# A second order for the loads and for TensorE's work ahead of a recurrence: W2's A2 quarters first, x's first rows in four batches between them, biases behind the products of W1

## The chip, the cores and the metric

The kernel runs on one core of a Trainium2 chip. The metric is the device time of one execution in microseconds (us), the median of several runs.

## The reference

x is 4 x 512 x 256 (batch, time, width), cond is 4 x 256, all f32. Cut to what matters:

```python
# layer 0: factors of rank 8 drawn from cond, one set for each batch row
c = (cond - mean) / sqrt(var + 1e-5) * ln_gamma + ln_beta
h = gelu(c @ W1 + bias1)                       # W1 256 x 256
w = h @ W2 + bias2                             # W2 256 x 8192 (8 MB)
a1, b1, a2, b2 = [t.reshape(B, 256, 8) for t in split(w, 4)]
u   = einsum('btd,bdr->btr', x, a2)
mid = gelu(x @ base_down + einsum('btr,blr->btl', u, b2))
v   = einsum('blr,btl->btr', b1, mid)
x2  = 2 * x + mid @ base_up.T + einsum('bkr,btr->btk', a1, v)
# layer 1: a recurrence over 512 steps
h_t = tanh(x2_t @ Wx + b + h_(t-1) @ Wh)       # h_(-1) = cond
out = x2 + h
```

## The kernel before

Each engine runs a program written out by hand in one order, and the programs meet at semaphores. There are two phases. The prologue builds all that the first step of the recurrence needs: the factors a2, b2, b1, a1 and the first 64 rows of time (T0) of x for all four batch rows, carried as far as x2 for the first 16 (the first 32 soon behind). The recurrence then runs 512 steps, each some 20 small TensorE products of the state with Wh in three bf16 parts (`state_products`), two tanh on ScalarE (ACT) and four small subtractions on VectorE (DVE). Later rows of x and the later blocks of layer 0 are worked in between the steps.

In the prologue, DMA loads are issued by SyncE (SP) in the order of its program. W2 is loaded in 16 quarters of types of 512 KB: type j (A1, B1, A2, B2), half c, and k, the half of the contraction. `w_products(j, c)` multiplies one half of one type: four products of 32 columns for k = 0, four for k = 1, each k behind its load's semaphore. Ahead of it a `bias_product(j, c)` puts bias2 into the same PSUM bank. The right-hand side `gRep` is gelu(c @ W1 + bias1), repeated for the ranks: it comes from the transposes of `cn` (the normalised cond), the copy `cT`, the products with W1 into `hpre`, two gelu on ACT, and a copy on DVE.

Behind each half DVE runs `keep_rank` (`wmul`, then `fac`), and `spread` makes b2d and a1d of it; A2 and B1 are turned by TensorE (`turn_factor`) and copied out as a2T and b1T. x's first rows are transposed (`first_transposes`) and copied by ACT to xT, and multiplied with base_down (`base_down_product`); u, the b2 product (out of b2d), gelu to mid0, base_up (`base_up_product`), v (`v0_product`), the a1 product (`a1_first_product`) and `make_x2` follow. `first_input_product` multiplies the first tile of x2 with Wx, and the last of them release the first tanh.

`keep_busy(n)` issues n products with zeros into columns that nobody reads; they stand where TensorE would otherwise wait. GpSimd (POOL) splits b, Wh and Wx into bf16 parts in that order (`parts`), each behind its load.

Of the kernel before, what the change touches and what calls it, by code (L numbers as in the profile page):

```python
# [32 lines left out]
def adaptive_lowrank_then_recurrence(nc, x, cond, base_up, base_down, ln_gamma, ln_beta, W1, bias1, W2,  # L33
# [24 lines left out]
    with ExitStack() as ctx:  # L58
# [16 lines left out]
        x_sb = sb("x_sb", [P, B, NTT, D])  # L75
# [69 lines left out]
        ld_x = [sem(f"ld_x{n}") for n in range(NTT)]  # L145
        ld_x_more = sem("ld_x_more")
# [74 lines left out]
        PLACE = {A2: 0, B2: 2, B1: 0, A1: 2}  # L221

        def wbank(j, c):
            return bank[PLACE[j] + c][:, 0:HC]
# [6 lines left out]
        def hpre(m):  # L231
            return (bank[7], bank[3])[m][:, D + B * m:D + B * (m + 1)]
# [61 lines left out]
        @block.sync  # L294
        def _(sp):
            w2v = W2.rearrange("(k p) (j n) -> k p j n", p=P, j=NTYPE)

            def load_x(n):
                sp.dma_start(x_sb[:, :, n], x[:, P * n:P * (n + 1)].rearrange("b p d -> p b d")).then_inc(ld_x[n], 16)

            def load_w2(j):
                for c in range(2):
                    for k in range(K2):
                        sp.dma_start(w2_sb[:, k, j, 2 * CH * c:2 * CH * (c + 1)],
                                     w2v[k, :, j, 2 * CH * c:2 * CH * (c + 1)]).then_inc(ld_w2[j][c][k], 16)
# [11 lines left out]
            sp.dma_start(x_sb[T0:P, :, 0], x[:, T0:P].rearrange("b p d -> p b d")).then_inc(ld_x_more, 16)  # L317
# [74 lines left out]
        def _(act):  # L392
# [3 lines left out]
            act.dma_start(bias1_sb[:], bias1.rearrange("(o n) -> o n", o=1)).then_inc(ld_bias1, 16)  # L396
            act.dma_start(b_rows[:], b_rnn.partition_broadcast(NPART)).then_inc(ld_b, 16)
            act.dma_start(bias2_sb[:], bias2.rearrange("(j c e n) -> e j c n", j=NTYPE, c=2, n=HC)).then_inc(ld_bias2, 16)
# [9 lines left out]
            for k in range(K2):  # L408
                act.wait_ge(tr_ready, k + 1)
                nc.scalar.copy(xT[:, k, :, 0:T0], bank[6 - k][:, 0:B * T0].rearrange("p (b t) -> p b t", b=B)).then_inc(  # L410
                    tr_moved, 1)
            for m in range(K2):
                act.wait_ge(hpre_ready, m + 1)
                nc.scalar.activation(gT[:, m, :], hpre(m), ACT.Gelu).then_inc(g_ready, 1)
            act.wait_ge(a2T_psum, 1)
# [29 lines left out]
            def fill_more_rows(h):  # L445
                act.wait_ge(rows_psum, h + 1)
                nc.scalar.copy(xT[:, :, 2 * h:2 * h + 2, T0:P],
                               more_rows_out(h).rearrange("p (k b t) -> p k b t", k=K2, b=2)).then_inc(rows_moved, 1)
# [40 lines left out]
        def _(dve):  # L489
            steps = [0]  # L490

            def then_wait(ins):
# [23 lines left out]
                                  bank[2][:, 0:K2 * B]).then_inc(cT_ready, 1)  # L516
# [126 lines left out]
        def _(pe):  # L643
            zeros_h = zeros[:].bitcast(BF16)
            pe.wait_ge(pool_step, 1)
            def keep_busy(n, spare=0):
                for _ in range(n):
                    nc.tensor.matmul(bank[spare][:, D:2 * D], zeros_h[:, 0:P], zeros_h[:, 0:D], start=True, stop=True,  # L648
                                     skip_group_check=True)

            keep_busy(WARM)
# [6 lines left out]
            keep_busy(12)  # L658

            def bias_product(j, c):  # L660
                nc.tensor.matmul(wbank(j, c), quadrant[:].rearrange("e i q -> e (i q)"),  # L661
                                 bias2_sb[:, j, c], start=True, stop=False, skip_group_check=True)
# [14 lines left out]

            def w_products(j, c):
                for k in range(K2):
                    pe.wait_ge(ld_w2[j][c][k], 16)  # L680
                    for e in range(NCH):
                        last = nc.tensor.matmul(wbank(j, c)[Q * e:Q * (e + 1), :],  # L682
                                                gRep[:, k].rearrange("p b r -> p (b r)"),
                                                w2_sb[:, k, j, HC * (NCH * c + e):HC * (NCH * c + e + 1)], start=False,
                                                stop=(k == K2 - 1), skip_group_check=True)
                last.then_inc(w_ready[j], 1)
# [24 lines left out]
            pe.wait_ge(ld_x[0], 16)  # L711
            first_transposes(0)
            first_transposes(1)
            keep_busy(4)
            pe.wait_ge(ld_bias1, 16)
            pe.wait_ge(h_ready, 2)
            for m in range(K2):
                nc.tensor.matmul(hpre(m), bias1_sb[:, P * m:P * (m + 1)], ident[0:1, 0:1].broadcast_to([1, B]),
                                 start=True, stop=False, skip_group_check=True)
            pe.wait_ge(cn_ready, 1)  # L720
            for k in range(K2):
                last = nc.tensor.transpose(bank[2][:, B * k:B * (k + 1)], cn[:, P * k:P * (k + 1)],
                                           ident[0:B, 0:B])
            last.then_inc(cT_psum, 1)
            keep_busy(4)
            pe.wait_ge(ld_down, 16)
            base_down_product(0, 0)
            pe.wait_ge(ld_w1, 16)
            pe.wait_ge(cT_ready, 1)
            for m in range(K2):  # L730
                for k in range(K2):
                    last = nc.tensor.matmul(hpre(m), w1_sb[:, k, P * m:P * (m + 1)], cT[:, k, :], start=False,
                                            stop=(k == K2 - 1), skip_group_check=True)
                last.then_inc(hpre_ready, 1)
            base_down_product(0, 1)
            for k in range(K2):
                base_down_product(1, k)
# [6 lines left out]
            bias_product(B2, 0)  # L744
            w_products(A2, 1)
            bias_product(B2, 1)
            keep_busy(4, 7)
            w_products(B2, 0)
            pe.wait_ge(fac_ready[A2], 2)
            turn_factor(A2, a2T_psum)  # L750
            for c in range(2):
                bias_product(B1, c)
# [5 lines left out]
            w_products(B2, 1)  # L758
            pe.wait_ge(ld_up, 16)
# [10 lines left out]
            w_products(B1, 0)  # L770
            for c in range(2):
                bias_product(A1, c)
# [5 lines left out]
            w_products(B1, 1)  # L778
            keep_busy(7, 7)
# [73 lines left out]
            def turn_more_rows(h):  # L853
                if h == 0:
                    pe.wait_ge(ld_x_more, 16)
                    pe.wait_ge(x2_next, 2)
                for k in range(K2):
                    for b in range(2):
                        e = 2 * k + b
                        last = nc.tensor.transpose(more_rows_out(h)[:, T0 * e:T0 * (e + 1)],  # L860
                                                   x_sb[T0:P, 2 * h + b, 0, P * k:P * (k + 1)], ident[T0:P, T0:P])
                last.then_inc(rows_psum, 1)

            def turn_rows(tile):
                n, b = unit_of(tile)
                if b == 0:
                    pe.wait_ge(ld_x[n], 16)
                for k in range(K2):
                    last = nc.tensor.transpose(rows_out(tile)[:, P * k:P * (k + 1)], x_sb[:, b, n, P * k:P * (k + 1)],  # L869
# [39 lines left out]
            def recurrence(pair, first, last):  # L909
                for s in range(PAIR):  # L910
# [6 lines left out]
                    else:  # L917
                        for m in range(K2):
                            first_input_product(0, m, 1).then_inc(z_ready, 1)
                        first_input_product(1, 0, 1)  # L920
                        bias_start(0, 1, 1)
                        for k in range(K2):
                            first_input_product(1, 1, k)
# [23 lines left out]

            pe.wait_ge(fac_ready[B1], 2)
            turn_factor(B1, b1T_psum)
            pe.wait_ge(bp_ready, 1)  # L950
# [5 lines left out]
            pe.wait_ge(b1T_ready, 2)  # L956
            for k in range(K2):
                v0_product(k)
            w_products(A1, 0)
            keep_busy(6, 7)  # L960
# [3 lines left out]
            w_products(A1, 1)  # L964
# [4 lines left out]
            bias_start(0, 1, 0)  # L969
            first_input_product(1, 0, 0)  # L970
            keep_busy(8, 7)
            pe.wait_ge(a1d_ready, 2)
            a1_first_product(1)
            keep_busy(3, 7)
# [26 lines left out]
```

## Time and profile before

| | us |
|---|---|
| median of three runs (526.53, 528.21, 528.35) | 528.21 |
| the profiled execution's own time | 527.65 |
| its span, first to last instruction | 525.9 |
| the prologue in it: to the products that release the first tanh | 37.6 |
| TensorE busy, as the profile shows it | 505.6 (96%) |
| DVE busy | 291.8 (55%) |
| ACT busy | 175.2 (33%) |

The device time lies 1.75 us above the span. TensorE's matmuls overlap, so that its busy share says only that few gaps stand between starts. Nearly all of the span is the recurrence, whose code the change leaves as it is but for its first step and the two transposes of more rows of x.

### The profile page before, as it was taken

The page shows a single profiled execution, that of the slowest core. Times are in us where ns is not written, and L with a number is a line of the kernel's source. Part 1 is how long each engine was busy: PE and PEld are TensorE (multiplying, and loading weights), DVE is VectorE, ACT ScalarE, POOL GpSimd, SP SyncE. Part 2 cuts the span into 40 slices and gives each one's busy share as a digit, 9 for nine tenths or more (in the row PEclk, how much of TensorE's full clock was granted, in tenths as well). Part 3 has the DMA queues.
Part 4 walks back from the last instruction along what each step waited for, and adds up shares of the span by engine and source line. Part 5 has one row for each costly group of instructions (what it writes and reads, how often), then busy time and mean ns, then how long its engine had stood idle before and what let it go on. Part 6 is the DMA issues. An engine that isn't in the chain of part 4 may idle for free.

```text
span 525.9 us, 33134 instructions
## 1 busy us (share of the span) xinstructions
PE 505.6 (96%) x14756; PEld 471.9 (90%) x14756; DVE 291.8 (55%) x2272; ACT 175.2 (33%) x1158; POOL 22.2 (4%) x35
## 2 busy tenths in 40 slices
PE   9999999999999999999999999999999999998885
PEld 6569999999999999999999999999999999998884
DVE  2535565565556556555655555555655655565553
ACT  3103333333333333333333333333333333333322
POOL 7350000000000000000000000000000000000000
PEclk9999999999999999999999999999999999999999
DMA  8970000000000000000000000000000000000000
GB/s 292 401 213 4 4 14 4 4 14 4 14 5 14 6 7 11 4 14 4 15 4 14 4 6 14 4 14 4 14 4 5 14 4 15 4 14 3 14 6 11
DMA packets 8114, 16.05 MB, mean 31 GB/s; under 512 B 500, under 2 KB 5924, under 8 KB 7972
## 3 DMA queue, kind: packets, MB, share of 16 engines
q1 hardware_dynamic: 7904, 13.90, 7.8%
q8 instruction: 115, 1.88, 1.5%
q14 instruction: 27, 0.22, 0.1%
q10 hardware_dynamic: 68, 0.05, 0.0%
HBM read 11.85 MB, written 2.10 MB: 27 GB/s over the span
## 4 chain that ended last, share of the span: by engine, by line
PE 94%; ACT 3%; issue 1%; DVE 1%; DVEq 0%; POOL 0%; POOLq 0%
PE bank L881 64%; PE bank L801 7%; PE bank L845 4%; PE bank L826 3%; ACT h_ring L462 3%; PE bank L850 2%; PE bank L840 2%; PE bank L821 2%; PE bank L831 2%; PE bank L648 2%; PE bank L682 2%; PE bank L810 1%; PE bank L661 1%; PE bank L785 1%; PE bank L869 1%
## 5 line engine op out<-in xcount | busy, mean ns | idle before, releaser
L881 PE MATMUL bank<-h_ring,whp 128*128 128x52 bf16 x6132 | 243.3, 186 | 13.2 <-ACT h_ring L462 13.2
L544 DVE TENSOR_TENSOR r_ring<-h_ring 128x4 f32<-128x4 f32 x1022 | 136.6, 164 | 205.7 <-ACT h_ring L462 203.2
L462 ACT ACTIVATE h_ring<-bank 128x4 f32<-128x4 f32 x1024 | 142.1, 174 | 320.3 <-PE bank L881 312.5
L881 PE MATMUL bank<-r_ring,whp 128*128 128x52 bf16 x4096 | 220.5, 185 | 0.0
L881 PEld LDWEIGHTS bank<-h_ring,whp 128*128 128x128 bf16 x6132 | 187.9, 96 | 34.2 <-ACT h_ring L462 25.8
L881 PEld LDWEIGHTS bank<-r_ring,whp 128*128 128x128 bf16 x4096 | 174.6, 96 | 0.0
L881 PE MATMUL bank<-l_ring,whp 128*128 128x52 bf16 (+1 forms) x2048 | 157.4, 178 | 0.0
L548 DVE TENSOR_TENSOR l_ring<-r_ring 128x4 bf16<-128x4 f32 x1024 | 136.2, 162 | 0.0
L881 PEld LDWEIGHTS bank<-l_ring,whp 128*128 128x128 bf16 x2048 | 122.5, 96 | 0.0
L801 PE MATMUL bank<-xp,wxp 128*128 128x32 bf16 x1488 | 63.0, 176 | 0.0
L801 PEld LDWEIGHTS bank<-xp,wxp 128*128 128x128 bf16 x1488 | 50.5, 96 | 0.0
L845 PE MATMUL bank<-mid,upT 128*128 128x128 f32 x120 | 28.1, 316 | 0.0
L826 PE MATMUL bank<-xT,down_sb 128*128 128x128 f32 x112 | 26.2, 316 | 0.0
L785 PE MATMUL bank<-ones,b3h 128*128 128x32 bf16 x128 | 22.4, 176 | 0.0
L845 PEld LDWEIGHTS bank<-mid,upT 128*128 128x128 f32 x120 | 17.9, 188 | 0.0
L826 PEld LDWEIGHTS bank<-xT,down_sb 128*128 128x128 f32 x112 | 16.7, 188 | 0.0
L592 DVE TENSOR_TENSOR y_sb<-x2T,h_ring 128x64 f32<-128x64 f32 x64 | 15.4, 283 | 0.6 <-ACT h_ring L462 0.6
L840 PE MATMUL bank<-mid,b1T 128*128 128x128 f32 x60 | 14.0, 316 | 0.0
L850 PE MATMUL bank<-v_sb,a1d 128*128 128x128 f32 x60 | 14.0, 316 | 0.0
L821 PE MATMUL bank<-xT,a2T 128*128 128x128 f32 x56 | 13.1, 316 | 0.0
L831 PE MATMUL bank<-u_sb,b2d 128*128 128x128 f32 x56 | 13.1, 316 | 0.0
L648 PE MATMUL bank<-zeros 128*128 128x256 bf16 x72 | 12.0, 319 | 1.0 <-POOL zeros L338 1.0
(123 smaller groups left out, 240.4 us busy)
## 6 DMA issues: line engine op xcount, KB each, us to landing
w_sb<-in_L_cond_W SPq DMA_DIRECT2D x16, 512.0 KB, 11.5
out<-o_sb SPq DMA_DIRECT2D x16, 128.0 KB
x_sb<-in_x SPq DMA_DIRECT2D x3, 512.0 KB, 15.2
x_sb<-in_x SPq DMA_DIRECT2D x2, 256.0 KB, 9.6
w_sb<-in_L_cond_W SPq DMA_DIRECT2D x1, 256.0 KB, 3.6
down_sb<-in_L_cond_base_down SPq DMA_DIRECT2D x1, 256.0 KB, 5.0
wh_sb<-in_L_cond_Wh SPq DMA_DIRECT2D x1, 256.0 KB, 11.1
up_sb<-in_L_cond_base_up SPq DMA_DIRECT2D x1, 256.0 KB, 11.3
```

The costliest lines, as they stand in the source:

```text
L462: nc.scalar.activation(h_ring[:, m, slot(pair, s), 0:B], zt, ACT.Tanh).then_inc(h_ready, 1)
L544: nc.vector.tensor_tensor(r_ring[:, k, q, 0:B], state_before(pair, s, k)[:, 0:B], state_hi_before(pair, s, k)[:, 0:B], ALU.subtract).then_ ...
L548: nc.vector.tensor_tensor(l_ring[:, k, q, 0:B], r_ring[:, k, q, 0:B], r_hi[:, k, q, 0:B], ALU.subtract).then_inc(l_ready, 1)
L785: nc.tensor.matmul(zbank(p, q, m)[:, 0:TC // 2], b3h[:, P * m:P * (m + 1)], ones[:], start=True, stop=False, skip_group_check=True)
L801: nc.tensor.matmul(zb, wxp[w][:, k, P * m:P * (m + 1)], rhs, start=False, stop=False, skip_group_check=True)
L821: ins = nc.tensor.matmul(columns(fill_out(tile, 0)), a2T[:, k].rearrange("p e q -> p (e q)"), xT[:, k, :, t0:t0 + BL], start=(k == 0), sto ...
L826: nc.tensor.matmul(columns(fill_out(tile, 1 + c)), down_sb[:, k, P * c:P * (c + 1)], xT[:, k, :, t0:t0 + BL], start=(k == 0), stop=False)
L831: nc.tensor.matmul(columns(fill_out(tile, 1 + c)), b2d[:, P * c:P * (c + 1)], u_sb[:], start=False, stop=True).then_inc(fmid_psum, 1)
L840: ins = nc.tensor.matmul(columns(fill_out(tile, 0)), b1T[:, k].rearrange("p e q -> p (e q)"), rhs, start=(k == 0), stop=(k == K2 - 1))
L845: nc.tensor.matmul(columns(fill_out(tile, 1 + c)), upT[:, k, P * c:P * (c + 1)], rhs, start=(k == 0), stop=False)
L850: nc.tensor.matmul(columns(fill_out(tile, 1 + c)), a1d[:, P * c:P * (c + 1)], v_sb[:], start=False, stop=True).then_inc(fup_psum, 1)
L881: return nc.tensor.matmul(zbank(p, q, m)[:, col0:col0 + n], whp[part][:, k, P * m:P * (m + 1)], rhs[:, 0:n], start=False, stop=stop, skip_ ...
```

## The change

The loads: W1 is now first, and laid out so that a partition takes two rows of W1 that lie together (the transposes of cn take every second column to match). The four quarters of A2 follow, each with one 64 KB batch of x's first rows behind it (`xa_sb`, 32 partitions for a batch row, two rows of time in each). Then come down, Wh, B2, up, Wx, B1, A1, and x's rows 64 to 127 (`xb_sb`). Before, x's first rows came first, then W1, down, A2, B2, Wh, up, B1, Wx, A1. On ACT's queue bias2's load stands ahead of b's.

```diff
-            sp.dma_start(x_sb[0:T0, :, 0], x[:, 0:T0].rearrange("b p d -> p b d")).then_inc(ld_x[0], 16)
-            sp.dma_start(w1_sb[:], W1.rearrange("(k p) n -> p k n", p=P)).then_inc(ld_w1, 16)
+            sp.dma_start(w1_sb[:], W1.rearrange("(p k) n -> p k n", p=P)).then_inc(ld_w1, 16)
+            for b in range(B):
+                load_w2_half(A2, b // 2, b % 2)
+                sp.dma_start(xa_sb[T0 // 2 * b:T0 // 2 * (b + 1)], x[b, 0:T0].rearrange("(q r) d -> q r d", r=2)).then_inc(
+                    ld_xa, 16)
             sp.dma_start(down_sb[:], base_down.rearrange("(k p) n -> p k n", p=P)).then_inc(ld_down, 16)
-            load_w2(A2)
+            sp.dma_start(wh_sb[:], Wh.rearrange("(k p) n -> p k n", p=P)).then_inc(ld_wh, 16)
             load_w2(B2)
-            sp.dma_start(wh_sb[:], Wh.rearrange("(k p) n -> p k n", p=P)).then_inc(ld_wh, 16)
             sp.dma_start(up_sb[:], base_up.rearrange("(k p) n -> p k n", p=P)).then_inc(ld_up, 16)
+            sp.dma_start(wx_sb[:], Wx.rearrange("(k p) n -> p k n", p=P)).then_inc(ld_wx, 16)
             load_w2(B1)
-            sp.dma_start(wx_sb[:], Wx.rearrange("(k p) n -> p k n", p=P)).then_inc(ld_wx, 16)
             load_w2(A1)
...
             def first_transposes(k):
-                for b in range(B):
-                    last = nc.tensor.transpose(bank[6 - k][:, T0 * b:T0 * (b + 1)], x_sb[0:T0, b, 0, P * k:P * (k + 1)],
-                                               ident[0:T0, 0:T0])
+                for r in range(2):
+                    last = nc.tensor.transpose(bank[6 + k][:, P * r:P * (r + 1)], xa_sb[:, r, P * k:P * (k + 1)],
+                                               ident[:])
```

On TensorE x's transposes move from before the products of W1 to behind A2's second half, and the products with base_down behind them, on both sides of A2's turning. The products with bias1 stand behind W1's, B2's second bias stands ahead of A2's second half, and the biases of B1 and A1, which now have columns of their own in the banks of A2 and B2, go ahead of A2's turning (the last of them just behind it). base_up's products come straight behind the b2 products; B1's two halves follow them. `w_half_products` splits a half at k: fillers or other products stand between. The fillers change in number at most places. ACT does its two gelu ahead of x's two copies.

The first place is TensorE's program from the first fillers on. zeros marks fillers, ident,x_sb (after: ident,xa_sb) x's transposes, ident,bias_sb bias1, ident,cn the transposes of cn, cT,w_sb the products with W1, xT,down_sb those with base_down, bias_sb,quadrant bias2, and w_sb,gRep those with W2. Before:

```order
L648 MATMUL bank<-zeros 128x256 x12
L669 MATMUL bank<-ident,x_sb 128x64 x8
L648 MATMUL bank<-zeros 128x256 x4
L718 MATMUL bank<-ident,bias_sb 128x4 x2
L722 MATMUL bank<-ident,cn 128x4 x2
L648 MATMUL bank<-zeros 128x256 x4
L675 MATMUL bank<-xT,down_sb 128x256
L732 MATMUL bank<-cT,w_sb 128x4 x4
L675 MATMUL bank<-xT,down_sb 128x256 x3
L661 MATMUL bank<-bias_sb,quadrant 128x256 x2
L682 MATMUL bank<-w_sb,gRep 32x256 x8
```

And now:

```order
L662 MATMUL bank<-zeros 128x256 x11
L730 MATMUL bank<-ident,cn 128x4 x2
L662 MATMUL bank<-zeros 128x256 x3
L739 MATMUL bank<-cT,w_sb 128x4 x2
L743 MATMUL bank<-ident,bias_sb 128x4
L739 MATMUL bank<-cT,w_sb 128x4 x2
L743 MATMUL bank<-ident,bias_sb 128x4
L662 MATMUL bank<-zeros 128x256
L674 MATMUL bank<-bias_sb,quadrant 128x256 x2
L694 MATMUL bank<-w_sb,gRep 32x256 x8
```

Eight transposes and four products with base_down have left the stretch ahead of W2's first products.

The second place is TensorE's program from A2's second half to the u product (xT,a2T). ident,fac is the turning of A2. Before, between A2's two halves stands one bias product, and behind the second:

```order
L661 MATMUL bank<-bias_sb,quadrant 128x256
L648 MATMUL bank<-zeros 128x256 x4
L682 MATMUL bank<-w_sb,gRep 32x256 x8
L691 MATMUL bank<-ident,fac 32x128 x8
L661 MATMUL bank<-bias_sb,quadrant 128x256 x2
L755 MATMUL bank<-xT,a2T 128x256 x2
```

Now:

```order
L682 MATMUL bank<-ident,xa_sb 128x128 x4
L674 MATMUL bank<-bias_sb,quadrant 128x256 x3
L688 MATMUL bank<-xT,down_sb 128x256 x2
L707 MATMUL bank<-ident,fac 32x128 x8
L688 MATMUL bank<-xT,down_sb 128x256 x2
L674 MATMUL bank<-bias_sb,quadrant 128x256
L694 MATMUL bank<-w_sb,gRep 32x256 x8
L774 MATMUL bank<-xT,a2T 128x256 x2
```

x's work and two more bias products have come in here.

The third place is from the turning of B1 (ident,fac) to the first a1 product (v_sb,a1d). mid,b1T is the v product; b3h, h_start, r_ring and l_ring are the bias and the state products of the first step. Before, with the last short rows of the states left out:

```order
L691 MATMUL bank<-ident,fac 32x128 x8
L785 MATMUL bank<-ones,b3h 128x32 x2
L881 MATMUL bank<-h_start,whp 128x52 x12
L881 MATMUL bank<-r_ring,whp 128x52 x6
...
L702 MATMUL bank<-mid,b1T 128x128 x2
L682 MATMUL bank<-w_sb,gRep 32x256 x8
L648 MATMUL bank<-zeros 128x256 x6
L708 MATMUL bank<-v_sb,a1d 128x128
```

Now:

```order
L707 MATMUL bank<-ident,fac 32x128 x8
L694 MATMUL bank<-w_sb,gRep 32x256 x4
L718 MATMUL bank<-mid,b1T 128x128 x2
L694 MATMUL bank<-w_sb,gRep 32x256 x4
L801 MATMUL bank<-ones,b3h 128x32 x2
L895 MATMUL bank<-h_start,whp 128x52 x12
...
L694 MATMUL bank<-w_sb,gRep 32x256 x4
L662 MATMUL bank<-zeros 128x256
L724 MATMUL bank<-v_sb,a1d 128x128
```

A1's first half now goes ahead of the first step's state products, in two pieces around the v product.

## Rows read from the trace of the kernel before

**Rows 1.** The page: the span, and TensorE's granted clock in 40 slices.

```profile
span 525.9 us, 33134 instructions
...
PEclk9999999999999999999999999999999999999999
```

**Rows 2.** The chain that ended last, 0 to 40 us: start us, us, what.

```profile
4.89 2.06 PE bank L648 x12
6.94 0.64 PE bank L669 x8
...
9.76 0.79 PE bank L732 x8
10.54 1.40 PE bank L675 x6
11.95 1.06 PE bank L661 x4
13.00 1.00 PE bank L682 x16
14.00 0.62 PE bank L661 x2
...
17.79 0.44 PE bank L691 x16
...
19.29 1.06 PE bank L755 x4
20.35 1.04 PE bank L682 x16
...
22.33 0.75 DVE b2d L531
...
23.13 0.70 PE bank L767 x2
23.82 0.44 PE bank L648 x4
...
26.32 1.09 PE bank L698 x8
27.41 1.04 PE bank L682 x16
...
29.48 0.64 PE bank L691 x16
...
30.27 0.62 PE bank L881 x24
30.89 0.53 PE bank L702 x4
...
32.49 0.44 DVE wmul L524
...
33.40 0.30 DVE a1d L531
...
33.84 0.46 PE bank L708 x2
...
37.57 0.86 PE bank L790 x6
```

**Rows 3.** DVE in order of time: start us, us, line, operation.

```profile
5.81 0.50 DVE L507 TENSOR_TENSOR cn<-cn,beta_sb 4x256 f32<-4x256 f32 x1
...
19.48 1.01 DVE L531 TENSOR_TENSOR b2d<-fac,qmask 128x128 f32<-128x128 f32 x1
```

**Rows 4.** POOL in order of time, with the wait ahead and its releaser.

```profile
18.50 0.61 POOL L362 CAST whp<-wh_sb 128x512 bf16<-128x512 f32 x1 [5.83 <-DMA wh_sb<-in_L_cond_Wh]
...
25.17 0.62 POOL L362 CAST wxp<-wx_sb 128x512 bf16<-128x512 f32 x1 [2.25 <-DMA wx_sb<-in_L_cond_Wx]
```

**Rows 5.** The issue of A1's last quarter (16.9 to 17.1 us), and its landing.

```profile
L304 SPq DMA_DIRECT2D w_sb<-in_L_cond_W x1: 1335/1335/1335, 15.8 to 15.8; - x1
...
DMA to landing us min/median/max: 15.7/15.7/15.7
```

More of the change, by code:

```diff
@@ L144, in adaptive_lowrank_then_recurrence @@
         ld_bias2 = sem("ld_bias2")
-        ld_x = [sem(f"ld_x{n}") for n in range(NTT)]
-        ld_x_more = sem("ld_x_more")
+        ld_xa = sem("ld_xa")
+        ld_xb = sem("ld_xb")
+        ld_x = [sem(f"ld_x{n}") for n in range(1, NTT)]
         ld_down = sem("ld_down")
@@ L414, in _ @@
                 nc.scalar.activation(gT[:, m, :], hpre(m), ACT.Gelu).then_inc(g_ready, 1)
+            for k in range(K2):
+                act.wait_ge(tr_ready, k + 1)
+                nc.scalar.copy(xT[:, k, :, 0:T0].rearrange("p b (q r) -> p r b q", r=2),
+                               bank[6 + k][:, 0:B * T0].rearrange("p (r b q) -> p r b q", r=2, b=B)).then_inc(tr_moved, 1)
             act.wait_ge(a2T_psum, 1)
@@ L676, in base_down_product, with w_half_products @@
                                  start=(k == 0), stop=False, skip_group_check=True)
+            def w_half_products(j, c, k):
+                pe.wait_ge(ld_w2[j][c][k], 16)
+                for e in range(NCH):
+                    last = nc.tensor.matmul(wbank(j, c)[Q * e:Q * (e + 1), :], gRep[:, k].rearrange("p b r -> p (b r)"),
+                                            w2_sb[:, k, j, HC * (NCH * c + e):HC * (NCH * c + e + 1)], start=False,
+                                            stop=(k == K2 - 1), skip_group_check=True)
+                if k == K2 - 1:
+                    last.then_inc(w_ready[j], 1)
             def w_products(j, c):
                 for k in range(K2):
[L680 to L686, printed above, removed]
+                    w_half_products(j, c, k)
             def turn_factor(j, done):
@@ L709, in a1_first_product @@
                                  stop=True, skip_group_check=True).then_inc(up_psum, 1)
[L711 to L719, printed above, removed]
+            keep_busy(11)
             pe.wait_ge(cn_ready, 1)
             for k in range(K2):
[L722 removed]
+                last = nc.tensor.transpose(bank[5][:, D + B * k:D + B * (k + 1)], cn[:].rearrange("b (p k) -> b k p", k=K2)[:, k],
                                            ident[0:B, 0:B])
             last.then_inc(cT_psum, 1)
[L725 to L727 removed]
+            keep_busy(3)
             pe.wait_ge(ld_w1, 16)
+            pe.wait_ge(h_ready, 2)
             pe.wait_ge(cT_ready, 1)
@@ L731, in _ @@
                 for k in range(K2):
[L732 to L737, printed above, removed]
+                    nc.tensor.matmul(hpre(m), w1_sb[:, k, P * m:P * (m + 1)], cT[:, k, :], start=(k == 0), stop=False,
+                                     skip_group_check=True)
+                if m == 0:
+                    pe.wait_ge(ld_bias1, 16)
+                nc.tensor.matmul(hpre(m), bias1_sb[:, P * m:P * (m + 1)], ident[0:1, 0:1].broadcast_to([1, B]),
+                                 start=False, stop=True, skip_group_check=True).then_inc(hpre_ready, 1)
+            keep_busy(1)
             pe.wait_ge(ld_bias2, 16)
@@ L758, in _ @@
             w_products(B2, 1)
+            keep_busy(2)
             pe.wait_ge(ld_up, 16)
@@ L854, in turn_more_rows @@
                 if h == 0:
-                    pe.wait_ge(ld_x_more, 16)
+                    pe.wait_ge(ld_xb, 16)
                     pe.wait_ge(x2_next, 2)
                 for k in range(K2):
[L858 to L861, printed above, removed]
+                    last = nc.tensor.transpose(more_rows_out(h)[:, P * k:P * (k + 1)], xb_sb[:, h, P * k:P * (k + 1)],
+                                               ident[:])
                 last.then_inc(rows_psum, 1)
@@ L919, in recurrence @@
                             first_input_product(0, m, 1).then_inc(z_ready, 1)
[L920 to L923, printed above, removed]
+                        for m in range(K2):
+                            first_input_product(1, m, 1)
                     if TURN <= s < TURN + K2 and not first:
@@ L946, in recurrence @@
                         output_transpose(pair, n)
+            w_half_products(B1, 1, 0)
+            keep_busy(4, 6)
+            w_half_products(B1, 1, 1)
+            keep_busy(9, 6)
             pe.wait_ge(fac_ready[B1], 2)
             turn_factor(B1, b1T_psum)
+            w_half_products(A1, 0, 0)
+            pe.wait_ge(b1T_ready, 2)
+            for k in range(K2):
+                v0_product(k)
+            w_half_products(A1, 0, 1)
             pe.wait_ge(bp_ready, 1)
@@ L955, in _ @@
             state_products(0, 0)
[L956 to L960, printed above, removed]
+            w_half_products(A1, 1, 0)
+            keep_busy(1, 7)
             pe.wait_ge(v0_ready, 1)
```

88 lines of the change are left out of this document (50 added, 38 removed).

## The prediction

> **What bounds the kernel now.** I read the page first. The span is 525.9 us and TensorE's clock is granted in full in every slice [rows 1], so nothing is to be had from the clock over the whole. Then the chain of work that ended last, over its first 40 us: the reader is to see that it runs down TensorE's program almost without a break, fillers (L648) and all, and that DVE is in it at three places only, the longest the one that ends in b2d [rows 2]. (An f32 product leaves two records, so x16 is eight products.) The last chain of the prologue ends at 37.57, where the products start that release the first tanh [rows 2]. So the prologue is bound by the sum of TensorE's program in its order, not by a transfer: A1's last quarter, the last load that it needs, is issued at 15.8 and lands 15.7 later, at 31.5 [rows 5], while the half that uses it begins after 34.30 (33.84 and 0.46) [rows 2]. After 37.57 come 488 us of recurrence whose steps depend on each other; a prologue that is shorter by a microsecond shortens the run by a microsecond, and nothing else in the change touches them.
>
> TensorE gets almost the same work as before: eight transposes of 64 rows become four of 128 (as many columns), no product is dropped, and the fillers fall from 72 to 67, which is 5 x 0.11 = 0.55 us at 0.44 for four [rows 2]. Anything more must come from waits and fillers no longer standing on TensorE's path to the last chain: A1's last half, its `keep_rank`, a1d, the a1 product, x2. So I follow the new program from point to point, with each group's length from the row of its like.
>
> **Start to gRep.** cn is ready at 5.81 + 0.50 = 6.31 [rows 3]. Eleven fillers instead of twelve end near 6.8 (twelve filled 4.89 to 6.94) [rows 2]; the transposes of cn can start there, not behind 6.94 + 0.64 of x's transposes, four fillers and bias1. W1 (256 KB, now first) is of no concern: before, it was second. cn's transposes, DVE's copy of them (I take 0.5 together, from the order of the short f32 groups in rows 2) and three fillers bring W1's products to 7.4. They take 0.79, and the two bias1 products behind them 0.2 each, as much as a product of W1 [rows 2]: 8.7 at the end, against 9.76 + 0.79 = 10.55. gRep is 1.8 earlier. TensorE then has one filler, a wait and two A2 biases (1.06) [rows 2] and reaches A2's first half at **10.0 instead of 13.00** [rows 2]. The 3.0 are x's transposes (0.64) and base_down (1.40 for three of four) that have moved, and fillers.
>
> **A2 to u.** A2's first half takes 1.0, the pair of B2 biases 1.06 (one alone was 0.62), so the second half starts at 12.1 (before 14.00 + 0.62 = 14.62) and ends at 13.1. Behind it the moved work comes back: transposes 0.5 (at most their 0.64), three biases 0.43 each and 0.1 for a change of kind, 1.4; two base_down products 0.95 (1.40 for three); A2's turning 0.5 (0.44 and the change); two more base_down 0.95; a bias 0.45; B2's first half 1.0; u 1.06 [rows 2]. 13.1 + 6.8 = 19.9, and some changes of kind at 0.1 make it 20.2 to 20.4. **B2's second half started at 20.35** [rows 2] **and starts there now.** What was won is spent, but two A1 biases (the group of 1.06 that stood before base_up) are already paid. Waits here are covered: `keep_rank` of A2's second half ends near 14.0, two microseconds before its turning, and ACT's two copies to xT, whose interleaved form no row shows (I take once to twice the 0.44 of a DVE pass over as many columns, `wmul` [rows 2]), before 15.4. Nothing that another engine needs is queued behind these copies but a2T's, due at 16.5.
>
> **b2d.** Two fillers and the transposes of up bring the first b2 product to 22.1, 0.3 later than before, and the second to 23.05, against 23.13 with its wait [rows 2]. What it waits for is b2d's second half. DVE's two spreads took 1.01 and 0.75, and a1d, the same operation on the same shape, 0.30 [rows 2, 3]. The long ones lie beside POOL's splitting of Wh (from 18.50), the short one beside none that reads [rows 4]. The Trainium skill (SBUF — State Buffer, "Who interferes with whom") says that a DVE operation with two SBUF inputs and a GpSimd operation that reads SBUF hold one port pair in turn, each for its whole length; the three durations agree. It matters now because the loads move: Wx lands behind B2 and up. The stream passes 256 KB in about 0.65 us (Wh's wait ended at 18.50 and Wx's at 25.17 for 2,560 KB between them) [rows 4]; with 2,048 KB of B1 behind Wx and no longer ahead of it, Wx lands near 19.9, and POOL, done with Wh by 17.5, splits Wx from 19.9 to 24.3, over both spreads. So the second still ends near 22.6 to 23.1. I take 22.6: that costs nothing, since TensorE gets there at 23.05.
>
> **base_up and B1.** Behind the second b2 product (0.54, without the wait's start) and four fillers 0.44, base_up starts near 24.1 (gelu covered) and takes 1.09; B1's first half follows at 25.2, its second in two quarters of 0.5 with four fillers (0.5) between, ending at 27.8. Before, that half ended at 27.41 + 1.04 = 28.45 [rows 2]. Gain 0.6; the two A1 biases are gone from here, the fillers take half of it back. DVE needs 0.9 and the reading of PSUM 0.4; nine fillers cover it, so the turning of B1 starts at **29.0 instead of 29.48** [rows 2].
>
> **A1.** Behind the turning: a quarter of A1 (0.45), a wait for b1T of 0.1, v (0.53 and a change, 0.6), the other quarter (0.45). A1's first half ends at 31.1; `keep_rank` starts at 31.4 and a1d is ready 33.40 + 0.30 - 32.49 = 1.2 later, 32.6; the a1 product starts at **32.7 instead of 33.84** [rows 2]. Here the other gain lies: the state products of the first step, 0.62 [rows 2], are behind A1's first half and not ahead of it. They fill the wait that fillers filled. A1's last quarter runs from 33.45 (0.39 of a1, three fillers), 1.9 us after its landing of 31.5 if that stays [rows 5]; a1d's second half is ready at 35.4, TensorE's products with Wx and six fillers end there too. x2 is ready and the last chain starts at **36.3 to 36.4 instead of 37.57**, 1.2 earlier. That chain is then shorter: the first step has one Wx product (0.22 of the 0.86 for three, less the wait) and one bias fewer behind it, 0.25. The rest of the first pair: four transposes of 64 rows in each of two steps become two of 128, as near nothing as rows 2 can tell.
>
> **Sum:** 1.2 + 0.25 = 1.45 us off 527.65, the profiled execution's own time, 526.2. The median shown is 0.56 above that execution, so 528.21 - 1.45 = **526.8**. It is 0.3%, and differences under about 0.5% (2.6 us) can't be told from none in this kernel.
>
> **The rivals.**
> 1. The spread meets a long POOL operation (0.12). POOL's second subtraction on Wx would start near 22.5; if the load is 0.2 us earlier, or POOL gets the port pair first, b2d is ready 1.2 later, near 23.8, and all behind slips by 0.7 to 0.8. By the Trainium skill's rule above that is a whole operation's wait. Gain 0.7: 527.5. For it: 1.01 us for the first spread in rows 3. Against: in rows 2 the second lost only 0.45.
> 2. Nothing is gained (0.10): an unforeseen change of kind (0.1 to 0.2 each, and the program has five more of them) eats it all; 528.2, perhaps 528.5.
> 3. The loads become the bound and the kernel is slower (0.10). The four 64 KB batches go to 32 partitions each, no row has a transfer of this kind, and the Trainium skill (DMA: Bandwidth & Descriptors, "Bandwidth") calls transfers of 64 KB and less dominated by overhead. A1's last quarter then lands late. It decides from 33.5 on (2.0 later than 31.5), and the run is slower than before from 35.0, since 1.45 was won; at 36.5, 1.25 us for each batch, it is 528.21 + 1.5 = 529.7. Against: the bytes ahead of it are the same, x's first rows are no more than before, and the queue has many transfers in hand.
> 4. The clock falls (0.08). The clock is at half for the first fillers (0.17 each in the group at 4.89 against 0.11 in that at 23.82) [rows 2] and full later. Between 6.8 and 9.0 TensorE would now do tiny products with four fillers where it had x's transposes and twelve. The 0.17 is a mix of 0.11 and its double, so the slow stretch at the start ended a little past 6. If the clock went to half at 7 for as long again, some 5 us, half of that work's time, 2.5 us, is lost against the forecast: 529.3. Against: tiny products also stood at 9.76 for 0.79 with no fall. The Trainium skill (TensorE: Matmul & The Clock Gate, "Part 1: The HAM clock gate") has the clock hang on how busy TensorE has just been; by the rows, it stays.
>
> **How the numbers follow.** The forecast, 526.8 with its own range of 526.0 to 527.7, has 0.60. Executions of the same kernel lay from 526.53 to 528.35, and a median of three may be 0.8 off, so the range for 8 in 10 is 524.9 to 528.6: it takes in rivals 1 and 2, and leaves out most of 3 and 4. Faster by over 0.5% (under 525.6): a quarter of the forecast, 0.14. Slower by over 0.5% (above 530.85): half of rivals 3 and 4 at their far ends, 0.08. Within 0.5%: the rest, 0.78.
>
> **What would show it.** In the changed trace: W2's first product near 10.0 and B2's second half near 20.3; the second b2 product at 23.1 without a wait for DVE; the turning of B1 at 29.0; the a1 products at 32.7 and 35.5; the last chain at 36.3, the first state products of the next step 1.45 earlier. A wait on a load at A2's or A1's quarters proves rival 3, a b2d of a microsecond or more rival 1, fillers at 0.21 behind 7 us rival 4. The prediction is wrong if the clock's rise comes at another time, or if the changed order brings waits between engines that I count as covered.

## The result: slower, and the profile after

| | before | after |
|---|---|---|
| median of 18 runs, us | 527.37 (526.16 to 528.35) | 534.47 (527.41 to 537.47) |
| mean granted clock of a run | 0.996 to 0.999 (19 later runs) | 0.974 to 0.995 |
| the profiled execution: time, span | 527.65, 525.9 | 529.02, 527.1 |

The medians stand as 1.0135 to 1. The ratio with an interval, 1.0095 [1.0073, 1.0117], leaves out six of the 18 runs as disturbed; the runs below show that what disturbs them is the change's own effect, so it is a lower bound. I had forecast 526.8 in a range of 524.9 to 528.6, and gave the mechanism that decided it, a fall of TensorE's clock, 0.08.

The page of the kernel after, its span and TensorE's granted clock in 40 slices:

```profile
span 527.1 us, 33111 instructions
...
PEclk8899999999999999999999999999999999999999
```

The first two slices are at 8 where those of before were at 9 [rows 1]: the clock is lost in the first 26 us. The stretches of the prologue one by one (us; then busy time and count of PE, PEld, DVE, ACT, POOL; granted clock; DMA share; GB/s):

```profile
4.00:7.00 3.00, 2.45 (x20) 1.71 (x18) 2.12 (x8) 2.15 (x5) 0.31 (x1) 1.00 0.99 306
7.00:10.00 3.00, 2.86 (x18) 2.38 (x17) 0.30 (x2) 0.35 (x2) 1.52 (x4) 1.00 1.01 352
10.00:13.00 3.00, 3.00 (x21) 1.52 (x20) 0.85 (x2) 0.00 (x0) 2.72 (x4) 0.58 1.07 363
13.00:16.00 3.00, 3.00 (x21) 1.08 (x20) 0.13 (x1) 0.00 (x0) 2.76 (x5) 0.50 1.04 414
16.00:19.00 3.00, 3.00 (x12) 2.12 (x11) 0.71 (x2) 0.77 (x2) 2.79 (x4) 0.78 1.05 378
19.00:22.00 3.00, 3.00 (x29) 1.69 (x32) 0.29 (x1) 0.27 (x1) 2.28 (x3) 1.00 1.03 407
```

From a little after 10 to a little after 17 us the clock stands at half (1.2 GHz for 2.4), while TensorE is busy without a gap. (It had stood idle for 0.55 us between 4 and 7 and for 0.14 between 7 and 10, as the rows show; whether that brings the fall, e9 below answers.) And the chain that ended last, with the groups that answer to those of rows 2:

```profile
9.20 1.06 PE bank L674 x4
10.26 1.61 PE bank L694 x16
11.87 2.00 PE bank L674 x4
13.87 1.86 PE bank L694 x16
15.73 1.05 PE bank L682 x4
16.78 1.78 PE bank L674 x6
18.56 1.06 PE bank L688 x4
...
23.94 1.00 PE bank L694 x16
...
26.57 0.43 PE bank L787 x2
...
32.05 0.67 PE bank L707 x16
...
35.99 0.33 PE bank L724 x2
...
39.61 0.86 PE bank L806 x8
```

The first bias pair takes 1.06 and the next, the same two products, 2.00; a half of W2 takes 1.00 at 23.94, and 1.61 and 1.86 here. Against their lengths at full clock (1.06 and 1.00 from this view; 0.59 for the transposes and 1.49 for the three biases from the chain of e6_bias_rows below) the five groups from 10.26 on lose 0.61 + 0.94 + 0.86 + 0.46 + 0.29 = 3.2 us. My forecast had the last chain at 36.3; 36.3 + 3.2 = 39.5, and it starts at 39.61. In other runs the clock stays low for longer: the run of 537.47 has a mean of 0.974; 2 x 0.026 x 527 is about 27 us at half clock.

The mean of a run has to be read with care. In the trace of e7_tail_only below, whose mean is 0.996, the clock is full up to 518 us and at half only at the very end, when TensorE has nothing left to do:

```profile
521.00:523.00 2.00, 0.00 (x0) 0.00 (x0) 0.00 (x0) 0.00 (x0) 0.00 (x0) 0.50 0.14 37
```

The trace of e6 has the same mean, and there 3.4 us of half clock lie in the prologue. So a mean of 0.996 or more, which all runs of the kernel before have, leaves room for one short spell, and only lower means tell of a longer one.

### The profile page after: what moved, and what is told of

Its sections match the earlier page's. It is cut to its first block, busy times and chain, and to the rows that moved or that the text cites. A ratio compares the mean times of both kernels' runs of the same rounds, so it can differ in the third digit from the quotient of the medians.

```text
span 527.1 us, 33111 instructions
## 1 busy us (share of the span) xinstructions
PE 507.2 (96%) x14743; PEld 471.4 (89%) x14743; DVE 289.4 (55%) x2272; ACT 175.4 (33%) x1158; POOL 21.9 (4%) x35
## 4 chain that ended last, share of the span: by engine, by line
PE 94%; ACT 3%; issue 1%; DVE 1%; DMA 0%; DVEq 0%; ACTq 0%
PE bank L895 63%; PE bank L817 7%; PE bank L861 4%; PE bank L842 3%; ACT h_ring L475 3%; PE bank L866 2%; PE bank L856 2%; PE bank L837 2%; PE bank L847 2%; PE bank L694 2%; PE bank L826 1%; PE bank L674 1%; PE bank L662 1%; PE bank L801 1%; PE bank L883 1%
## 5 line engine op out<-in xcount | busy, mean ns | idle before, releaser
L861 PEld LDWEIGHTS bank<-mid,upT 128*128 128x128 f32 x120 | 17.9, 188 | 0.0
L801 PEld LDWEIGHTS bank<-ones,b3h 128*128 128x128 bf16 x128 | 12.1, 95 | 0.8 <-issue 0.8
```

Of the source, the lines that this page charges most:

```text
L801: nc.tensor.matmul(zbank(p, q, m)[:, 0:TC // 2], b3h[:, P * m:P * (m + 1)], ones[:], start=True, stop=False, skip_group_check=True)
L861: nc.tensor.matmul(columns(fill_out(tile, 1 + c)), upT[:, k, P * c:P * (c + 1)], rhs, start=(k == 0), stop=False)
```

## The experiments

In all of them the time beside a kernel is its median with its lowest and highest run, and the kernel before was run on the same chip (527.38, 527.2 and 527.01 in the three sets).

**More or other fillers.** e1_more_fill:

```diff
-            keep_busy(11)
+            keep_busy(16)
...
+                keep_busy(2)
-            keep_busy(1)
+            keep_busy(5)
```

> The change with more fillers ahead of W2's first products: 16 for 11 ahead of cn's transposes, two behind each half of W1's products, 5 more behind these (9 for 1 in all, four of them inside). Theory A (TensorE did too little between the first fillers and W2's first products, so the clock falls to half a little after): the clock stays at full from its first rise in most runs (mean clock 0.998 or more), and the time is that of my forecast plus the fillers on the path, 8 x 0.11 = 0.9 us: 527.5 to 528. Rival B (what brings the fall is the stretch behind, 10 to 17 us, of bias products with 4 rows and products with 32 columns): no change in the falls, 534 and a spread of several us. Rival C (fillers that do not start an accumulation don't count as work): no change either, or little.

Measured: 532.96 (526.81 to 536.36, four runs). One run kept its clock (0.999) and took 526.81; three did not. (The slowest shows a mean clock of 0.841, far below what its time would fit; I have no explanation for it.) Theory A in that simple form is gone: more fillers in front don't cure it. The clean run says what the path is worth, though: it is 0.6 below the kernel before, with 13 fillers more than the change.

e2_fill_start:

```diff
-            keep_busy(11)
+            keep_busy(11, first=True)
...
-            keep_busy(3)
+            keep_busy(3, first=True)
...
-            keep_busy(1)
+            keep_busy(1, first=True)
```

> The change, but the 11, 3 and 1 fillers start their accumulation, as all fillers of the kernel before did. Rival C: the falls go and the time is 526 to 527. Theory A and rival B: as the change, a median near 534 with single runs from 527 to 537 and a mean clock from 0.974 to 0.995.

Measured: 533.22 (532.21 to 535.97, four runs), mean clock 0.979 to 0.986. Rival C is out.

e3_before_few:

```diff
-            keep_busy(12)
+            keep_busy(9)
...
-            keep_busy(4)
...
-            keep_busy(4)
```

> The kernel before with fewer fillers early on: 9 for 12 ahead of x's transposes, none for the four behind them, none for the four behind cn's transposes (11 fewer). Theory A: the clock now falls in some or most runs of this kernel too, 529 to 537 with a mean clock down to 0.975 or so. Rivals B and C: the clock stays, and the path is up to 0.8 us shorter, 526.5 to 527.4.

Measured: 526.95, but in two heaps: six runs from 526.03 to 527.62, and four from 532.4 to 533.0, each of the four with a mean clock of 0.985. One of the six, 527.62, has 0.995, the others 0.996 or more. The kernel before, at 0.996 or more in all 19 runs beside it, stands close to the edge: eleven fillers off, and it falls in four runs of ten. Theory A had expected that, and rivals B and C had not: what stands in front counts too.

e4_fill_late:

```diff
-            keep_busy(1)
+            keep_busy(9)
             pe.wait_ge(ld_bias2, 16)
```

> The change with 9 fillers for 1 behind W1's products, just ahead of W2's bias products, and nothing else. Theory A: the falls get rarer or go; with none the time is 526.8 + 8 x 0.11 = 527.7, and if the stretch from 4 to 9 us counts too, some runs stay at 529 to 534. Rival B and C: as the change, near 534 or 535.

Measured: 532.65 (526.71 to 536.89, ten runs); one run kept its clock. Eight fillers just ahead of the stretch in which it falls move the median by less than 2 us.

**What stands in the stretch.** Taking fillers away in front brings the fall in some runs, and adding them there does not cure it. So the work behind them must count for little. There are two suspects: the bias2 products, which contract over 4 rows (the reader sees 4*128 in the profile), now in pairs and five of them where the clock is low; and the dense products of x that are gone from there. e5_fill_all is e1 with more:

```diff
             w_products(A2, 0)
+            keep_busy(4)
             for c in range(2):
                 bias_product(B2, c)
+            keep_busy(4)
             w_products(A2, 1)
+            keep_busy(4)
```

> The change with the fillers of e1_more_fill (which did not cure it) and four more in each of three places: on both sides of the pair of B2's biases and behind A2's second half. Path: 8 + 12 fillers, 20 x 0.11 = 2.2 us over a run without a fall (which the best runs of e1 and e4 put near 525.9), 528.1. Theory D (the clock falls where the work of a few microseconds is mostly bias products of 4 rows and products of a few columns; before, dense products of x stood among them): falls get rare, median near 528. Rival E (it is the number of columns in any stretch, and fillers of zeros do not stand in for products with data): falls stay, 533 to 537.

Measured: 529.28 (528.32 to 536.96, seven runs): five runs at 528.3 to 529.4 with a mean of 0.995 to 0.998, two at 536.5 and 537.0. The profiled run, one of the five (529.36), still has 3.4 us at half clock (0.60 over 10 to 13 us, 0.83 over 13 to 16). So twenty-five fillers more than the change keep the spell short or away in most runs, and cost more than the change was worth: all seven are slower than 527.2, the median of before. Rival E's half on zeros is out: they count, if there are enough. Its other half, the number of columns, this run can't test, since fillers bring columns; e6 and e9 below, with as many columns each, do.

e6_bias_rows:

```diff
-        bias2_sb = sb("bias2_sb", [NCH, NTYPE, 2, HC])
+        bias2_sb = sb("bias2_sb", [P, NTYPE, 2, HC])
...
-        quadrant = sb("quadrant", [NCH, NCH, Q])
+        quadrant = sb("quadrant", [P, NCH, Q])
...
+            nc.vector.memset(bias2_sb[:, A2:B2 + 1], 0.0).then_inc(bias_zero, 1)
...
-                nc.tensor.matmul(wbank(j, c), quadrant[:].rearrange("e i q -> e (i q)"),
-                                 bias2_sb[:, j, c], start=(j in (A2, B2)), stop=False, skip_group_check=True)
+                rows = P if j in (A2, B2) else NCH
+                nc.tensor.matmul(wbank(j, c), quadrant[0:rows].rearrange("e i q -> e (i q)"),
+                                 bias2_sb[0:rows, j, c], start=(j in (A2, B2)), stop=False, skip_group_check=True)
```

> The change, but the bias2 products of A2 and B2 contract over 128 rows, of which 124 are zeros, instead of over 4: as many instructions and columns, the same sums. DVE zeroes the rows at the start, and bias2's load is the last on ACT's queue. Theory D in its narrow form (products that use 4 rows of the array do not count as work): the falls go or get rare, 526 to 527.5. If rows of zeros count for nothing, or if the cause lies elsewhere: falls as in the change, 533 to 536.

Measured: 526.14 (525.62 to 527.61, ten runs), 0.9991 [0.998, 1.0002] of before: 8.3 us less than the change, for four products whose rows are filled with zeros. The interval takes in 1, so this cures the change but is not shown to be faster than before. Its chain, where the clock is down in the first two groups only:

```profile
9.43 1.64 PE bank L678 x4
11.07 1.86 PE bank L698 x16
12.93 1.06 PE bank L678 x4
13.99 1.00 PE bank L698 x16
14.99 0.59 PE bank L686 x4
15.58 1.49 PE bank L678 x6
```

e9_rows_control sets `rows = NCH` in the code above and leaves the rest of e6 as it is:

```diff
-                rows = P if j in (A2, B2) else NCH
+                rows = NCH
```

> All of e6_bias_rows (the zeroed rows, bias2's load last on ACT's queue) but the products themselves, which contract over 4 rows again as in the change. If the rows are what keeps the clock (theory D, narrow form): falls as in the change, median 532 to 535. If the later load or DVE's work at the start did it: 526 to 527.5, as e6.

Measured: 534.74 (529.12 to 537.23, four runs), mean clock 0.974 to 0.992. So neither the zeroing nor the later load did it, but the rows. The products of bias2 in e6:

```profile
L678 PE MATMUL bank<-bias_sb,quadrant x16: 374/379/634, 9.3 to 20.0; 128*128 128x256 f32 x8, 4*128 4x256 f32 x8
```

and in e9:

```profile
L678 PE MATMUL bank<-bias_sb,quadrant x16: 374/629/791, 9.3 to 26.4; 4*128 4x256 f32 x16
```

The group of e6 mixes both forms, so the price of the rows is better read where the clock was full throughout: the biases of A2 and B2 in e12_tail_rows (128 rows) and in e7_tail_only (4 rows), both described below:

```profile
L665 PE MATMUL bank<-bias_sb,quadrant x8: 379/379/483, 10.9 to 14.8; 128*128 128x256 f32 x8
L661 PE MATMUL bank<-bias_sb,quadrant x8: 374/374/478, 11.4 to 15.4; 4*128 4x256 f32 x8
```

At full clock the 124 rows of zeros cost 5 ns of 374. The stretches of e6:

```profile
7.00:10.00 3.00, 3.00 (x19) 2.52 (x19) 0.36 (x2) 0.35 (x2) 2.67 (x5) 0.90 1.02 314
10.00:13.00 3.00, 3.00 (x20) 1.07 (x19) 0.00 (x0) 0.00 (x0) 2.70 (x4) 0.53 1.08 341
13.00:16.00 3.00, 3.00 (x26) 1.83 (x27) 1.68 (x4) 0.60 (x2) 2.17 (x3) 1.00 1.03 409
```

and of e9:

```profile
7.00:10.00 3.00, 3.00 (x18) 2.38 (x17) 0.38 (x2) 0.35 (x2) 2.66 (x5) 0.85 1.03 321
10.00:13.00 3.00, 3.00 (x20) 1.17 (x18) 0.00 (x0) 0.00 (x0) 2.60 (x4) 0.50 1.06 351
13.00:16.00 3.00, 3.00 (x16) 1.56 (x16) 0.84 (x2) 0.00 (x0) 1.86 (x3) 0.50 1.03 411
16.00:19.00 3.00, 3.00 (x18) 1.72 (x11) 0.84 (x2) 0.78 (x2) 2.28 (x3) 0.50 1.05 379
19.00:22.00 3.00, 3.00 (x8) 1.89 (x8) 0.00 (x0) 0.00 (x0) 1.22 (x2) 0.50 1.03 408
22.00:30.00 8.00, 8.00 (x64) 4.22 (x63) 1.88 (x6) 0.27 (x1) 6.81 (x5) 0.74 1.04 396
```

In both the clock falls between 9 and 10 us, behind W1's products of four columns. What the rows change is how long it stays down: back before 13 in e6, past 22 in e9. What makes it fall at that point these two runs do not separate; e3 and e8 bear on it. PE is busy for the whole of every one of these rows, in e9 from 1 us to 30, so its busy share tells nothing of this, and the short idle times of the change's own trace are not needed for the fall.

e10_few_rows puts e6's edit into e3_before_few:

```diff
+                rows = P if j in (A2, B2) else NCH
+                nc.tensor.matmul(wbank(j, c), quadrant[0:rows].rearrange("e i q -> e (i q)"),
+                                 bias2_sb[0:rows, j, c], start=True, stop=False, skip_group_check=True)
```

> The kernel before with 11 fewer fillers (e3_before_few, whose clock fell in 4 of 10 runs, to 532.4 to 533.0, and whose others took 526.0 to 527.6), with A2's and B2's bias products over 128 rows. Theory D: the falls go, or last for one short spell, and all runs lie between 525.8 and 528. Rival (the falls of e3 come from what was taken away in the first 10 us alone): some runs at 532 to 533 again.

Measured: 526.09 (525.23 to 528.12, ten runs); none of the runs near 532 that e3 had four of. Four of ten against none of ten could by itself be chance; together with e6 and its control it says the same. Short spells are left here too: the profiled run, the slowest (528.12, outside the range I gave), is at half clock for 3.4 us (0.54 over 10 to 13 us, 0.89 over 13 to 16).

**What each part of the order is worth.** e8_x_front:

```diff
             for b in range(B):
-                load_w2_half(A2, b // 2, b % 2)
                 sp.dma_start(xa_sb[T0 // 2 * b:T0 // 2 * (b + 1)], ...
...
+            load_w2(A2)
...
-            keep_busy(3)
...
+            first_transposes(0)
+            first_transposes(1)
...
-            keep_busy(1)
+            pe.wait_ge(ld_down, 16)
+            for m in range(K2):
+                for k in range(K2):
+                    base_down_product(m, k)
```

> The change, but x's four batches and down are loaded between W1 and A2, x's transposes stand for the three fillers behind cn's, and the four products with base_down ahead of W2's biases in place of one filler; ACT copies x ahead of the two gelu. The rest, tail and placed biases, is the change's. Theory D: dense products are back in the first 12 us, so few or no falls, and a path as long as the change's without falls: 526.0. Rival: the pairs of bias products still bring the fall, 532 to 536.

Measured: 528.44 (524.95 to 535.12, ten runs). x's work ahead of W2 brings the median down by 6 us from the change's, so its leaving, with the loads and the order of ACT that go with it here, was a part of the cause; but seven runs of ten still lose 1.5 us or more. The pairs of biases are where the change put them, and there are only the 11 fillers in front where before had 20; which of the two is behind these falls is not shown. e11_x_front_rows adds the 128 rows to it:

```diff
+                rows = P if j in (A2, B2) else NCH
```

> e8_x_front with A2's and B2's bias products over 128 rows. e8 ran at 525.0 to 525.8 without a fall and at 527.4 to 535.1 with. Theory D: most runs at 525 to 526, none above 529. Rival: a spread as in e8.

Measured: 527.33 (524.71 to 528.64, ten runs). The long falls are gone (none above 529), but I had expected most runs at 525 to 526. Two took less than 525; the other eight took 526.5 or more, with mean clocks of 0.992 to 0.995: shorter falls are still there. The profiled run (526.5) shows where. Up to 16 us its clock is full, and then:

```profile
16.00:19.00 3.00, 3.00 (x34) 1.53 (x36) 0.52 (x2) 0.27 (x1) 2.38 (x3) 0.81 1.03 395
19.00:22.00 3.00, 3.00 (x24) 1.50 (x20) 1.52 (x4) 0.00 (x0) 0.95 (x2) 0.62 1.04 404
```

Just ahead, from 15.2 to 17.9, stand the four biases of A1 and B1, which still contract over 4 rows, and the turning of A2. That these bring this later fall fits theory D, but no run filled their rows.

e7_tail_only takes the kernel before to its b2 products, and the change's order from there:

```diff
-            w_products(B1, 0)
-            for c in range(2):
-                bias_product(A1, c)
             pe.wait_ge(upT_ready, 1)
...
-            w_products(B1, 1)
-            keep_busy(7, 7)
+            w_products(B1, 0)
...
+            w_half_products(B1, 1, 0)
+            for c in range(2):
+                bias_product(A1, c)
+            w_half_products(B1, 1, 1)
+            keep_busy(7, 6)
```

> The kernel before, loads and order alike, up to the b2 products, and from there the change's order: base_up ahead of B1's halves, A1's first half in two quarters around v and ahead of the first step's state products, the first step without its second bias and one product. A1's biases stand between the quarters of B1's second half. Theory D: the first 20 us are those of before, so no falls; the terms of the forecast behind B1 (1.1 at the a1 product, 1.2 at the last chain, 0.25 in the first step) are all there: 527.4 - 1.4 = 526.0. Rival: the tail by itself brings falls or has no gain, 527.4 or more.

Measured: 526.0 (525.28 to 526.62, ten runs), 0.9977 [0.9967, 0.9986] of before: as expected, 1.2 us of the 1.4. Its chain:

```profile
4.88 1.56 PE bank L648 x12
...
22.89 0.70 PE bank L771 x2
...
29.12 0.69 PE bank L695 x16
...
33.08 0.33 PE bank L712 x2
...
36.70 0.86 PE bank L790 x8
...
37.86 0.59 PE bank L881 x24
```

The first a1 product stands at 33.08 for 33.84, the last chain at 36.70 for 37.57 [rows 2]. Not all of that is the tail's: the twelve first fillers happened to take 1.56 for 2.06, and the second b2 product, from which the programs differ, is already at 22.89 for 23.13. The last line is the state products of the next step; in the kernel before they are

```profile
39.20 0.59 PE bank L881 x24
```

From the second b2 product to them it is 14.97 us for 16.07: 1.10 is the tail's, 0.63 of it ahead of the last chain and 0.47 behind its start. The front of the order, the loads too, was not needed for this.

**A version that beats both.** e12_tail_rows is e7 with the 128 rows, and without the four fillers behind x's transposes and the four behind cn's:

```diff
             first_transposes(1)
-            keep_busy(4)
...
             last.then_inc(cT_psum, 1)
-            keep_busy(4)
...
+                rows = P if j in (A2, B2) else NCH
```

> e7_tail_only (526.0) with the eight fillers ahead of W1's products taken out and A2's and B2's bias products over 128 rows. Theory D: no lasting falls, and the eight fillers' 0.9 us come off as far as cn does not become the wait: 525.2 to 525.7. Rival: falls as in e3, some runs at 530 or more.

Measured: 524.68 (524.49 to 525.24, five runs), 0.9963 [0.995, 0.9975] of before, 2.3 us less, and the narrowest spread of all, though of five runs only. It is below the 525.2 to 525.7 that I expected; the two groups of four fillers took 0.54 each in the chain of before, and the wait for b2d was shorter than in e7. The same kernel with the biases over 4 rows was not run. Its last chain starts at 35.62:

```profile
21.81 0.70 PE bank L773 x2
...
28.05 0.69 PE bank L699 x16
...
32.00 0.33 PE bank L716 x2
...
35.62 0.86 PE bank L792 x8
```

## Why the prediction was wrong

The step that failed is rival 4, the clock. I wrote "tiny products also stood at 9.76 for 0.79 with no fall" and "by the rows, it stays", and gave it 0.08. It fell: sixteen of the 18 runs have a mean of 0.992 or less, and the other two 0.995, below the lowest of before. I had looked only at what was left between 6.8 and 9.0 (and had set twelve fillers against the four there, where the program of before has eight there, 4 and 4). I had not asked the same of the stretch behind it, where the change puts pairs of 4-row biases between the halves of A2, with x's dense products and four fillers gone. In the kernel before, base_down's products (1.40) [rows 2] stood between the short products of W1 and the first biases. e3 shows how thin the cover was, and e6, e9 and e10 that products over 4 rows are what keeps the clock down once it has fallen. The sign that I had named, fillers at 0.21, could not show it: no filler stands in the slow stretch, and the one at 0.21 (at 8.99) ran at full clock. The halves of W2 at 1.61 and 1.86 for 1.00 show it.

The price was also too low. I had one spell at half clock, 2.5 us. The profiled run lost 3.2, and the median run some 8 (534.47 against the 526.14 of e6), since a clock that is down in such a stretch stays down for a while (e9: past 22 us).

The rest of the sum held, in its own order:
- gRep and A2's first half: forecast 10.0, measured 10.26 in the chain; W1's two halves with their biases took 0.85 to 0.9 each, not 0.6. (My terms up to the end of bias1, 7.4 + 0.79 + 0.4, make 8.6 and not the 8.7 that I wrote.)
- From A2's second half to B2's second half: forecast 8.25; measured 23.94 - 13.87 = 10.07, of which 0.86 + 0.46 + 0.29 are the clock. 8.46 is left.
- b2d (rival 1): the spreads took 0.29 each, not the 1.01 and 0.75 of before [rows 2, 3]. TensorE did not wait:

```profile
23.86 0.29 DVE L544 TENSOR_TENSOR b2d<-fac,qmask 128x128 f32<-128x128 f32 x1
...
25.93 0.29 DVE L544 TENSOR_TENSOR b2d<-fac,qmask 128x128 f32<-128x128 f32 x1
```

  But the fall had pushed them some 3 us back, to where POOL was at its last operations on Wx and at a memset, so this is no test of the rival. In e6, with less delay, they took 0.68 and 0.53 beside POOL's operations on Wx, and the second b2 product 0.63 for 0.43: rival 1 was there, at up to 0.2 us and not 0.7.

- From B2's second half to the last chain: forecast 16.0, measured 39.61 - 23.94 = 15.67.
- Rival 3, the loads: no wait for a load of x or W2 stands in TensorE's chain. A1's last quarter was issued at 16.4 and landed 14.9 later, at 31.3, against 31.5.
- The sum of 1.45: in the change's chain the state products of the next step start at 40.78, 1.58 later than the 39.20 of before; without the 3.2 of the clock they are 1.6 earlier. The part for the first step was too small: from the last chain's start to them it is 1.17 for 1.63, 0.46 and not 0.25. In run times the whole is not shown: e7's median is 1.2 below that of before, e6's 1.1, with short falls still in it. The one run of e4 that kept its clock (526.71, less 0.88 for the added fillers: 525.8) is the fastest of ten beside a median.

What stays open: why the clock falls where it does, behind W1's products, and in some runs and not in others. The load order by itself was not tried with the old order of TensorE, so whether it helps is not shown, only that nothing waited on it. Nor is it shown which of the changes, x's leaving, the fillers that went, or the pairing of the biases, weighs more; e8 gives 6 us for bringing x back (and the loads with it), e6 8.3 for filling the rows of the biases, and no run undoes the pairing alone.

## What to carry to other kernels

Before moving dense products out of the first tens of microseconds, list what is left in each stretch with the rows that each product uses, not its busy time: TensorE was at 3.00 of 3.00 in the stretches where its clock was lost. Where a small product (a bias over a few rows) has to stand in such a stretch, fill its rows with zeros; at full clock the product is not longer, and here it was worth 8 us where fillers needed 25 instructions and gave less. Run such a change many times and read each run's mean clock, knowing that it also counts the idle end of the run: the profiled run alone (529.02) would have shown less than half of the loss.

## What the runs showed of the hardware

- Bias products over 4 rows do less for the clock than the same products over 128 rows, 124 of them zeros: with nothing else changed the clock is back before 13 us with 128 rows and stays down past 22 with 4, and the medians are 526.14 and 534.74.
- TensorE busy without a gap does not keep its clock: in e9 PE is busy for the whole of 1 to 30 us, and at half clock from about 9 to 26.
- The granted clock of the profile does not show the slow start. In the trace of before it reads 1.00 from 1 to 10 us, while the first sixteen fillers take 3.59 us, 0.22 each, against 0.11 later.
- The Trainium skill (TensorE: Matmul & The Clock Gate, "Part 1: The HAM clock gate") has the clock follow how busy TensorE has been. The runs agree only if busy is not what the profile shows as busy.
- b's small load (3 KB) was waited for until 8.25 instead of 5.47 in the trace of before, though it was issued at 2.55 instead of 2.44:

```profile
8.25 0.39 POOL L386 CAST b_part<-b_rows 3x256 bf16<-3x256 f32 x1 [3.94 <-DMA b_rows<-in_L_cond_b]
```

It stands behind bias2's on ACT's queue now, but that alone is not the cause: e8, with the same order on that queue and x's batches ahead of A2 on the other, has 5.78, and e6, with b ahead of bias2 and the change's loads, 6.01. Only both together made it late. It cost nothing here, since Wh's parts, done by 19.6, were not needed before 34; a chain with less room would have paid 2.8 us.
